# Chunked cross-attention on one core: 68 more idle waits at the head of the matmul program, and the masks of the first three rounds laid before the values

## What is computed

```python
def proj(t, W, b):
    t = t.transpose(0, 2, 1) @ W.T + b
    return t.reshape(N, nc, CHUNK, H, Dh)
qh, kh, vh = proj(q, Wq, bq), proj(k, Wk, bk), proj(v, Wv, bv)
scores = jnp.einsum('bnqhd,bnkhd->bnhqk', qh, kh) * scale
scores = scores + jnp.where(km[:, :, None, None, :] > 0, 0.0, NEG)
attn = jax.nn.softmax(scores, axis=-1)
out = jnp.einsum('bnhqk,bnkhd->bnqhd', attn, vh).reshape(N, T, C)
out = (out @ W_out.T + b_out).transpose(0, 2, 1) * masks
...
out = out + x
mu = jnp.mean(out, axis=2, keepdims=True)
var = jnp.mean(jnp.square(out - mu), axis=2, keepdims=True)
return (out - mu) * jax.lax.rsqrt(var + EPS)
```

## Time and profile before

| what | value |
|---|---|
| median of the runs shown | 1998.1 us (3 runs, 1996.77 to 2081.76) |
| the profiled execution: its time | 1996.5 us |
| its span, first to last instruction | 1994.7 us |
| busy: TensorE / VectorE / GpSimd / ScalarE | 95 / 86 / 74 / 65% |
| DMA data queue (q1), share of 16 engines | 72.0% |
| instruction queue (q8) | 320 packets, 5.24 MB |

### The profile page before, as it was taken

The page is one execution under the profiler, slowest core; times in us unless marked ns, Lnnn a source line. Parts: engine busy times, 40 slices in busy tenths (PEclk is TensorE's granted clock), DMA queues, the critical chain, the costliest instruction groups (busy, mean ns, idle before and its releaser), DMA issues.

```text
span 1994.7 us, 90619 instructions
## 1 busy us (share of the span) xinstructions
PE 1892.6 (95%) x40488; PEld 1581.5 (79%) x40488; DVE 1720.4 (86%) x1577; ACT 1303.3 (65%) x1792; POOL 1485.5 (74%) x1059
## 2 busy tenths in 40 slices
PE   6999999999999999999999999999999999999994
PEld 5888788888888888787888888788788878878883
DVE  4798889888888888888998888888888888888886
ACT  5567667666666676676676676666666666666662
POOL 4677778777777777777877777777777777777764
PEclk9999999999999999999999999999999999999997
DMA  5567777777777777777777777777777777777666
GB/s 161 151 174 210 208 216 210 212 214 205 212 217 208 204 215 212 204 217 205 215 210 215 215 210 208 217 205 213 217 203 208 212 210 206 211 200 221 192 173 199
DMA packets 242882, 409.60 MB, mean 205 GB/s; under 512 B 28992, under 2 KB 94784, under 8 KB 242496
## 3 DMA queue, kind: packets, MB, share of 16 engines
q1 hardware_dynamic: 242496, 403.82, 72.0%
HBM read 168.82 MB, written 67.11 MB: 118 GB/s over the span
## 4 chain that ended last, share of the span: by engine, by line
PE 93%; issue 4%; ACT 1%; DVE 1%; POOL 1%; DMA 0%; SPq 0%; DVEq 0%; POOLq 0%; ACTq 0%
PE proj_bank L310 38%; PE proj_bank L347 19%; PE proj_bank L368 18%; PE score_bank L387 10%; PE o_bank L424 9%; POOL prob L565 0%; DMA b_cols<-b_in 0%; ACT score_bank L478 0%; SPq L256 0%; POOL y L583 0%; ACT prob L486 0%; ACT q_f L499 0%; DMA prob_t<-squares 0%; DVE squares L681 0%; ACT o_hi L493 0%
## 5 line engine op out<-in xcount | busy, mean ns | idle before, releaser
L565 POOL TENSOR_TENSOR prob<-prob,recip 128x1024 f32<-128x1024 f32 x256 | 482.3, 1905 | 469.5 <-DVE recip L673 462.8
L508 ACT ACTIVATE k_f<-proj_bank,b_cols 128x512 f32<-128x512 f32 x256 | 176.7, 690 | 507.7 <-PE proj_bank L310 507.7
L654 DVE TENSOR_REDUCE row_max<-score_bank 128x32 f32<-128x2048 f32 x128 | 293.4, 2292 | 119.4 <-PE score_bank L387 118.6
L310 PE MATMUL proj_bank<-ctx_hi,w_lo 128*128 128x512 f32 x1024 | 322.8, 396 | 60.7 <-issue 60.7
L310 PE MATMUL proj_bank<-ctx_hi,w_hi 128*128 128x512 f32 x1024 | 337.9, 411 | 3.0 <-DVE ctx_lo L638 3.0
L573 POOL TENSOR_TENSOR ctx_lo<-ctx_raw,ctx_hi 128x512 fp32r<-128x512 f32 x255 | 326.3, 1301 | 12.5 <-ACT ctx_hi L466 12.5
L583 POOL TENSOR_TENSOR y<-y,x_raw 128x512 f32<-128x512 f32 x256 | 324.9, 1290 | 9.5 <-DVE y L699 9.5
L310 PE MATMUL proj_bank<-ctx_lo,w_hi 128*128 128x512 f32 x1024 | 323.5, 397 | 0.0
L665 DVE TENSOR_REDUCE sums<-prob 128x16 f32<-128x1024 f32 x256 | 308.5, 1206 | 4.1 <-ACT prob L486 4.1
L658 DVE TENSOR_TENSOR prob<-score_bank,row_max 128x2048 f32<-128x2048 f32 x128 | 293.3, 2292 | 4.4
L681 DVE STREAM_TRANSPOSE squares<-prob 128x2048 f32<-128x2048 f32 x128 | 294.6, 2301 | 0.9 <-POOL prob L565 0.9
(11 more groups left out here) (45 smaller groups left out, 3420.9 us busy)
## 6 DMA issues: line engine op xcount, KB each, us to landing
prob_t<-squares SPq DMA_DIRECT2D x1024, 128.0 KB
ctx_raw<-ctx SPq DMA_DIRECT2D x128, 512.0 KB, 4.8
x_raw<-x SPq DMA_DIRECT2D x128, 512.0 KB, 5.6
out<-y SPq DMA_DIRECT2D x128, 512.0 KB, 4.6
mask_all<-mask SPq DMA_DIRECT2D x128, 256.0 KB, 3.4
v_x<-v_f SPq DMA_DIRECT2D x256, 128.0 KB, 3.8
y<-w_in_t SPq DMA_DIRECT2D x1, 768.0 KB, 5.6
y<-w_out_t SPq DMA_DIRECT2D x1, 256.0 KB, 6.6
```

The lines of the kernel that those rows point to most:

```text
L310: last = pe.matmul(proj_bank[:, f, :], w[:, h, col + f * P:col + (f + 1) * P], c[:, n % 2, h, :], start=(a == 0 and h == 0), stop=(a == 2 ...
L565: pool.tensor_tensor(part, part, half(slots(recip[:, n % 2, :]), i), ALU.mult).then_inc(norm_done, 1)
L654: dve.tensor_reduce(row_max[:, :].rearrange("p (r c) -> p r c", c=CPB), scores_of, AX_X, ALU.max).then_inc(max_done, 1)
```

## The change

```diff
-LEAD = 102
+LEAD = 170
...
                 high_attention(p - 1)
-                values(p + 2, 0)
-                lay_negatives(p + 2, 0)
-                values(p + 2, 1)
-                lay_negatives(p + 2, 1)
+                if p < 1:
+                    lay_negatives(p + 2, 0)
+                    lay_negatives(p + 2, 1)
+                    values(p + 2, 0)
+                    values(p + 2, 1)
+                else:
+                    values(p + 2, 0)
+                    lay_negatives(p + 2, 0)
+                    values(p + 2, 1)
+                    lay_negatives(p + 2, 1)
```

## The result

The changed kernel takes **2044.4 us** (median of 4 runs, 2030.51 to 2052.36) against 2000.1 us for the kernel before (4 runs, 1996.77 to 2081.76): 1.022 times as long, 95% interval 1.0146 to 1.0293. It is slower; whether by more than 2% the interval leaves open. The run of 2081.76 us was in a slower state of the chip and is left out of the ratio. I had forecast 1951 us, faster, with a range to 1992. The profiled execution took 2052.36 us, 55.9 more than the one of before.

The account below looks back on a forecast made before the run. TensorE was taken to set the pace, stalling in even rounds at an instruction-block boundary. Terms -69.7 + 19 + 3 + 8 - 4 - 3 = -46.7 against 1996.5 us gave 1949.8, forecast 1951 us; range 1924 to 1992.

Parts of the forecast that it names:

- the block after odd 613: Fetch after the boundary at instruction 613 of odd rounds, counted from the first score load: 0.05 us a round, +3 us.
- two neighbours: Earlier boundaries used to estimate the fetch after odd 613: even 7, 3.2 us, and one behind x's load, 5.4 us.
- even 7: Earlier boundary at instruction 7 of even rounds, among the scores: 3.2 us from entering the block to having the next.
- a block held scores alone: Block from instruction 7 to 263 of even rounds, 2.1 us, too short to cover the next fetch; its removal saves 69.7 us.
- the sign of being wrong that I had named: An idle of over 1 us in every odd round before L368 or among the scores: a 4 us fetch is too slow.
- slower: Rival: fetch after odd 613 sits out x's load, 1.3 us stall, plus 1.4 after odd 357; about 2095 us, chance 0.05.
- odd 357: Boundary at instruction 357 of odd rounds, in L424; its 4.2 us block stalls 0.3 us in 62 rounds, +19 us.
- the stall moves and keeps its size: Rival: the two short blocks stall 0.6 us each on average, 74 us against 70; about 2003 us, chance 0.1.
- the removal at L310: TensorE's idle at L310's weight loads in even rounds, 1.16 us each, goes: -69.7 us.
- `o_lo`: Each fourth round, where VectorE closes a batch, TensorE waits 0.25 us for o_lo, 31 times: +8 us.
- Start, masks and the clock near 50: Start 0; masks ahead of values in three early rounds -4.0 us; half-clock stretch from 50.9 to 57.7 gone -3 us.
- The rival I had built on it, that blocks are not the cause: Even rounds' idle at L310 has another cause and stays; only start, masks and clock act: 1991 us, chance 0.1.

Follow-up runs that it names:

- the table: Changed kernel's new order with only the count of waits varied: 256 2113.0 us, 204 2040.2, 170 2044.4, 102 1983.9, 94 1968.8, 78 1932.9, 70 1931.6.

## Why the prediction was wrong

**The step that failed** is the term for the block after odd 613: "It leaves 0.9 us to spare. I take 0.05 us a round, **+3 us**, bounds 0 and 1.5." It measured 1.76 us a round, 107 us in sum, and is the only stall that matters. Two choices made it. First, from two neighbours I took even 7, with 3.2 us from entering a block to having its successor, because the load of x would be over. Halving x changed nothing: the load of x was never the criterion. Second, I treated the need as a property of the block, to be set against its length. The runs show a time of the round: the packet comes behind the last wait, at 14.7 to 15.4 on average, whether TensorE entered the block at 9.5, 10.7, 11.7 or, in the kernel before, at 14.6 (even 7). The 3.2 us read at even 7 were short because the block there is entered only after that wait. Seen so, the stalls of before and after have the same late packet, and moving the place where it is needed from 263 to 229 brings it 0.9 us nearer: 1.12 becomes 1.76, 0.64 of the 0.9. That a block held scores alone, whose removal was to be the gain, was not what made it stall: with 256 waits it holds most of L347 and all of L368 besides scores, lasts 6.4 us and stalls more. An idle of over 1 us among the scores was the sign of being wrong that I had named.

**The size even went past my bound**: 1.5 against 1.76, as the fetch needs 5.9 us from odd 613 to resumption against the 4.1 there are (of it 0.2 us is the time from landing to resumption, for which I had 1.2 and the median is 1.4). The rival *slower* had the right place, but 5.4 us, a stall of 1.3, from the load of x; its second half, 1.4 us after odd 357, did not come (0.13). Its time was 2095; the measured one lay between it and *the stall moves and keeps its size*, 2003.

**What held.** The stall lies where the boundary was computed, within one instruction, at each of the five counts of waits that have one, so the removal at L310, -69.7, was right as a term: 0.8 us is left of it. Odd 357: +19 forecast, 8.1 measured (10 of 61 rounds over 0.3 us). `o_lo`: +8 forecast, 11.5 - 4.1 = +7.4 on the loads in 28 rounds, but since the even rounds still stall, little of it reached their length; with 78 waits, where they do not, every fourth round costs that much and the row is 15.2. Start, masks and the clock near 50: -7 forecast, -8.2 measured, with the mask wait at 1.0 us as worked out. (That the slow matmuls of the first projection ran at the lower level I took from their pace alone: neither trace has a granted clock before 16.74 and 15.17 us.) TensorE's timeline at the start, against the earlier trace rows, has the first projection at 12.28, forecast 12.55, and the faster pace from the fourth pair on:

```profile
10.28 2.07 PE L399 MATMUL score_bank<-zero_rows 32*64 32x256 f32 x32 [10.28 <-issue]
12.28 1.22 PE L310 MATMUL proj_bank<-ctx_hi,w_hi 128*128 128x512 f32 x2
...
15.01 0.71 PE L310 MATMUL proj_bank<-ctx_hi,w_hi 128*128 128x512 f32 x2
```

**What was missing**: the clock. Stalls of 1.76 us on average were followed by twelve stretches at its lower level, +19 us; those of 1.12 us before by one, behind an idle of 1.55 us in the chain. The runs whose stall is 1.07 us or less (102 waits in the new order, 94, 78, 70) have none between 60 us and the tail. I had costed each stall at its own length.

**The rule.** A boundary here cost 1.1 us before and 1.8 us after in each even round. The Trainium skill, "Runtime: NRT & Kernel Launch", section Instruction fetch mechanics, calls the crossing "mostly hidden"; this case's rows bear that out for the blocks with a full 6.9 us, and contradict it for these. The rival I had built on it, that blocks are not the cause, is excluded by the table: only the count of waits differs in it, the time runs from 0.969 to 1.060, and the stall moves with the boundary. One reading that I set against the page was too strong, that packets start only after a block is entered: with 204 waits the packet asked for at odd 340 starts before TensorE's first weight load of that block in most rounds, by up to 0.9 us. It is still one block ahead, not eight.

## What to carry to other kernels

When a long written-out program stalls with no semaphore as the cause, count its instructions in blocks of a packet and find where in the loop each boundary falls; then read for each packet when in the round it comes, not only how long after its block was entered, since one whose block was entered early may still come behind a wait. Padding at the head moves all boundaries at once and costs 0.11 us for two waits: place them where the next block is needed late, in long instructions, and sweep a few counts on the chip, since a neighbouring boundary's cost does not carry over. Where a stall cannot be avoided, keep it short: the granted clock may fall behind a long one.

## What the runs showed of the hardware

A 16 KB instruction packet takes 0.9 to 1.5 us here in most cases and TensorE resumes 1.4 us after it lands (median; 1.2 to 1.6 in the changed kernel). Each packet belongs to one boundary. It starts anywhere from 0.9 us before (with 204 waits) to 6.9 us after (with 256) TensorE's first weight load of the block before the one it brings, and one that falls at the end of a round starts no sooner than 0.9 to 1.1 us after a semaphore wait that stands up to 70 instructions further on in the program. The length of the padding at the program's head alone is worth 9% of this kernel: 1931.6 us with 70 waits, 2113.0 with 256.
